# Banded attention: values projected once per block of 512 tokens and fetched back through DRAM, GpSimd placing them, and the output product given its own bank behind the turns

## The reference, cut to what matters

```python
x = layernorm(h)                       # [4, 1024, 128]
q, k, v = x @ Wq.T + bq, x @ Wk.T + bk, x @ Wv.T + bv     # 16 heads of 8
# row i sees its own chunk of 10 and the keys from i-25 up to the chunk's start
allowed = (j in chunk(i)) | ((j >= i - 25) & (j < chunk_start(i)))
p = softmax(q @ k.T * 8**-0.5 + where(allowed, 0, -1e30))
h = h + (p @ v) @ Wo.T + bo
```

## Time and profile before

| | |
|---|---|
| median of three runs | 2047.76 us (2047.59 to 2050.64) |
| the profiled execution's own time | 2046.14 us |
| its span in the profile | 2044.3 us |
| mean granted TensorE clock | 0.976 of full speed |
| attention A, first tile to the next layer's first instruction | 35.7 to about 246 us |
| busy share of the span, PE / DVE / ACT / POOL | 95 / 86 / 61 / 72 % |

### The profile page before, as it was taken

The page is one execution under the profiler, slowest core; times in us unless marked ns, Lnnn a source line. Parts: engine busy times, 40 slices in busy tenths (PEclk is TensorE's granted clock), DMA queues, the critical chain, the costliest instruction groups (busy, mean ns, idle before and its releaser), DMA issues. The chain is left out here.

```text
span 2044.3 us, 55129 instructions
## 1 busy us (share of the span) xinstructions
PE 1936.5 (95%) x22048; PEld 1290.8 (63%) x22048; DVE 1755.2 (86%) x2719; ACT 1239.2 (61%) x2213; POOL 1474.8 (72%) x1046
## 2 busy tenths in 40 slices
PE   4999889999879999999999999999999998899998
PEld 2666654444357777777777777777777776544443
DVE  5777788887679999999999999999999997788876
ACT  2455456666546666666666666666666665466665
POOL 2041035656449999999999999999999998256565
PEclk9999879999979999999999999999999999799999
DMA  7322258866230000000000000000000000487672
GB/s 184 120 72 72 70 108 146 149 118 137 48 114 10 17 10 16 11 14 13 9 18 10 13 14 13 14 10 17 6 10 6 10 6 2 86 152 155 133 138 51
DMA packets 99470, 117.44 MB, mean 57 GB/s; under 512 B 31920, under 2 KB 60976, under 8 KB 98288
## 3 DMA queue, kind: packets, MB, share of 16 engines
q1 hardware_dynamic: 97920, 113.42, 25.6%
q10 hardware_dynamic: 1296, 0.50, 0.1%
HBM read 96.32 MB, written 17.57 MB: 56 GB/s over the span
## 5 line engine op out<-in xcount | busy, mean ns | idle before, releaser
L1029 DVE TENSOR_REDUCE head_shift<-head_score 128x64 bf16<-128x1024 f32 x512 | 624.2, 1219 | 80.2 <-PE head_score L813 68.4
L986 ACT ACTIVATE head_ex<-head_score 128x1024 f32<-128x1024 f32 x512 | 524.7, 1025 | 183.4 <-PE head_score L835 181.7
L770 POOL TENSOR_TENSOR head_half<-head_ex 128x1024 f32<-128x1024 f32 x256 | 604.0, 2359 | 40.3 <-ACT head_ex L986 40.3
L1263 POOL TENSOR_TENSOR ffn_sw<-ffn_sg,ffn_wide 128x512 f32<-128x512 f32 x256 | 324.5, 1268 | 311.5 <-ACT ffn_sg L1374 300.2
L1036 DVE TENSOR_TENSOR head_ex<-head_ex,head_recp 128x1536 f32<-128x1536 f32 x256 | 446.7, 1745 | 4.3 <-ACT head_recp L958 4.3
L845 PE MATMUL head_den<-head_half,c_ident 128*128 128x128 f32 x3072 | 385.4, 275 | 2.4 <-POOL head_half L771 2.4
L845 PEld LDWEIGHTS head_den<-head_half,c_ident 128*128 128x128 f32 x3072 | 363.4, 192 | 6.0 <-POOL head_half L771 2.6
L777 POOL TENSOR_TENSOR head_ex<-head_ex,head_recip 128x512 f32<-128x512 f32 x256 | 328.5, 1283 | 21.5 <-ACT head_recip L960 13.8
L835 PE MATMUL head_score<-head_shift,c_identb 128*128 128x512 bf16 x1024 | 309.9, 384 | 18.1 <-DVE head_shift L1029 12.0
L813 PE MATMUL head_score<-att_b_HB,att_b_GR 96*128 96x256 f16 x2048 | 311.0, 274 | 0.5 <-ACT head_ex L986 0.5
L828 PE MATMUL head_outp<-head_ex,att_b_vs 128*32 128x128 f32 x8192 | 276.5, 276 | 0.6 <-DVE head_ex L1036 0.6
(11 more groups left out here) (255 smaller groups left out, 2545.4 us busy)
## 6 DMA issues: line engine op xcount, KB each, us to landing
ffn_wide<-pair_weights SPq DMA_DIRECT2D x256, 256.0 KB, 9.7
att_b_vs<-in_zero_f SPq DMA_DIRECT2D x2, 2176.0 KB, 9.3
a_keys<-band_parts_k SPq DMA_DIRECT2D x14, 295.5 KB, 2.6
att_a_HB<-a_keys SPq DMA_DIRECT2D x56, 73.9 KB
a_queries<-band_parts_q SPq DMA_DIRECT2D x14, 271.5 KB, 3.0
att_a_GR<-a_queries SPq DMA_DIRECT2D x14, 271.5 KB
b_queries<-head_parts_q SPq DMA_DIRECT2D x32, 96.0 KB, 1.6
att_b_HB<-b_queries SPq DMA_DIRECT2D x128, 24.0 KB
```

The source lines that it names most:

```text
L770: ch.link(pool.tensor_tensor(hf, e[:, 0:8, :], e[:, 8:16, :], ALU.add))
L986: act.activation(ex[:, kt % RING, :, h * QS:(h + 1) * QS], score[:, h, :, :].rearrange("p k (a w) -> p (k a) w", a=NH // 2), ACT.Exp, scal ...
L1029: dve.tensor_reduce(shift[:, h, :], score[:, h, :, :].rearrange("p k (a w) -> p w k a", a=NH // 2), AX.XY, ALU.max, negate=True).then_inc( ...
L1263: pool.tensor_tensor(sw[:, unit % 2, :], sg[:, unit % 2, :], wide[:, k % 2, i, :], ALU.mult).then_inc(sw_ready, 1)
```

## The change

- `values` is called once for a block of 512 tokens (128 columns of `xnT` as weights, 12 matmuls), for blocks 0 to 2 before the first tile and for blocks 3 to 7 in the turns of tiles 3, 6, 9, 12 and 15. The columns of `a_WvT` are reordered on the host, so that even and odd heads lie apart.
- ACT, between the exponentials and the copies of the turned ones, moves them to `v_rows` in SBUF, two instructions with zeros kept between the heads, and writes them to a DRAM tensor `v_dram` of 1 KB a token (ACT's queue). SP reads them back, two DMAs for a group, with 64 keys on 64 partitions and 12 windows in 512-byte pieces, into `v_windows`. POOL copies a tile's 512 elements on each of 128 partitions into `vw`. DVE's `place_values` and the per-tile `values` go.
- On PE, `project`, `turn_x` and `values` come before `turn`, and `output` comes last, into `bank_v`. `project` and `turn_x` no longer wait for `added`.
- `project` runs for 12 groups and not 14, and SP places 12. `place` waits for the group before's reads in front of its writes, not behind its own reads.
- POOL clears all three `HB`/`GR` buffers, adds the bias row block by block between placements, and scales and splits the later weights in 13 pieces (tiles 16 to 28 and 20 to 32), where it did it in four.
- Before the first tile: SP holds back input blocks 3 to 7 until the `a_` weights have landed, `normalise(2)` comes before the low part of the weights, and the bias row is made at the end of DVE's list.

```diff
 # sync
+            def place_windows(n):
+                first = n // NGRP * S + n % NGRP * GT * QT
+                sp.wait_ge(v_written, ONE + blocks_for(first + (WINDOWS - 1) * SUBQ + KWIN) * 16)
+                if n > 0:
+                    sp.wait_ge(v_placed, ONE + n * 32)
+                if n > 1:
+                    sp.wait_ge(v_done, ONE + (n - 1) * GT)
+                for e in range(2):
+                    rows = bass.AP(v_dram.tensor, first * 2 * E + e * E, [[2 * E, KWIN], [SUBQ * 2 * E, WINDOWS], [1, E]])
+                    sp.dma_start(v_windows[e * KWIN:(e + 1) * KWIN, n % 2, :, :], rows).then_inc(v_placed, 16)
...
-            clear(0)
+            sp.wait_ge(a_loaded, ONE + 4 * 16)
             for k in range(EARLY, NBLK):
                 load_x(k)
-            clear(1)
...
-            for n in range(2, B * NGRP + 2):
-                place(n, n % NGRP)
+            for n in range(2, GROUPS):
+                place(n)
+                place_windows(n)
 # gpsimd
+            def place_values(tile):
+                buf, n = tile % GT, tile // GT
+                pool.wait_ge(v_placed, ONE + (n + 1) * 32)
+                if tile >= GT:
+                    pool.wait_ge(att_ready, ONE + tile - GT + 1)
+                slots = vw[:, buf * NSUB * NG:(buf + 1) * NSUB * NG, :].rearrange("p s (r w) -> p s r w", w=16)
+                heads = v_windows[:, n % 2, buf * NSUB:(buf + 1) * NSUB, :].rearrange("p j (g r w) -> p (j g) r w", g=NG, r=2)
+                pool.tensor_copy(slots[:, :, 0:3:2, :], heads).then_inc(v_done, 1)
 # tensor: the turn
                     take_maximum(tile)
-                    values(b, (t + 1) * QT if t < NQT - 1 else S, tile + 1, bank_v)
-                    if out_tile(t) is not None and not (first and t == 0):
-                        output(b, t)
-                    turn(tile)
-                    if block_at(tile) is not None:
-                        pe.wait_ge(added, ONE + outs_before(b, t + 1))
-                        pe.wait_ge(low_ready, ONE + units_before(b, t))
-                        turn_x(block_at(tile))
-                    if t % GT < 2:
+                    if projects(b, t):
                         group = t // GT + 2
                         ahead = group // NGRP * S + group % NGRP * GT * QT
-                        pe.wait_ge(added, ONE + outs_before(b, t + 1))
                         pe.wait_ge(low_ready, ONE + units_before(b, t))
                         pe.wait_ge(xlow_ready, ONE + turned_before(tile))
                         project(b * S + (ahead + (0 if t % GT else LEFT)), KCOLS if t % GT else QCOLS, bank_q, t % GT)
+                    if block_at(tile) is not None:
+                        pe.wait_ge(low_ready, ONE + units_before(b, t))
+                        turn_x(block_at(tile))
+                    if values_at(tile) is not None:
+                        pe.wait_ge(added, ONE + outs_before(b, t) - (1 if t == 0 else 0))
+                        values(values_at(tile), bank_v)
+                    turn(tile)
+                    if out_tile(t) is not None and not (first and t == 0):
+                        output(b, t)
 # scalar
+            def take_values(k, bank):
+                if k > 1:
+                    act.wait_ge(v_written, ONE + (k - 1) * 16)
+                act.wait_ge(v_ready, ONE + k + 1)
...
+                for e in range(2):
+                    places = v_rows[:, k % 2, :, e, :].rearrange("p t (h w) -> p t h w", w=2 * D)[:, :, :, e * D:(e + 1) * D]
+                    heads = bank.rearrange("p (t e h d) -> p t e h d", t=TB, e=2, d=D)[:, :, e, :, :]
+                    last = act.activation(places, heads, ACT.Copy, scale=1 / ASCALE)
+                last.then_inc(v_taken, 1)
+                if k > 0:
+                    act.wait_ge(v_written, ONE + k * 16)
+                act.wait_ge(v_taken, ONE + k + 1)
+                rows = v_dram[LEFT + k * BLK:LEFT + (k + 1) * BLK, :].rearrange("(t p) e -> p t e", p=P)
+                act.dma_start(rows, v_rows[:, k % 2, :, :, :].rearrange("p t e w -> p t (e w)")).then_inc(v_written, 16)
...
+                    if values_at(tile) is not None:
+                        take_values(values_at(tile), bank_v[:, :])
```

More of the change, by code:

```diff
@@ L198, in block_at, with values_at, projects @@
             return EARLY + tile // GT if tile % GT == GT - 1 and EARLY + tile // GT < NBLK else None
+        def values_at(tile):
+            return EARLY + tile // GT - 1 if tile % GT == 0 and tile > 0 and EARLY + tile // GT - 1 < NBLK else None
+        def projects(b, t):
+            return t % GT < 2 and b * NGRP + t // GT + 2 < GROUPS
         def out_tile(t):
@@ L251, in _ @@
             sp.dma_start(whole("a_bo"), drams["a_bo"].partition_broadcast(P)).then_inc(out_loaded, 16)
-            for n in range(2):
-                place(n, n)
+            clear_rows(0, LEFT)
+            clear_rows(LEFT + T, VTAIL)
+            place(0)
+            sp.wait_ge(out_loaded, ONE + 5 * 16)
+            place_windows(0)
+            place(1)
+            place_windows(1)
             for name in LATE:
@@ L293, in project, with values @@
                 product(pe, bank[:, 0:cols], w, u, xh, xl).then_inc(qk_ready, 1)
-            def values(b, first, tile, bank):
+            def values(k, bank):
                 w = c["a_parts"]
-                pe.wait_ge(v_done, ONE + tile)
-                pe.wait_ge(xlow_ready, ONE + blocks_for(b * S + first + (NSUB - 1) * SUBQ + KWIN))
-                for j in range(NSUB):
-                    at = bass.ds(b * S + (first + j * SUBQ), KWIN)
+                pe.wait_ge(xlow_ready, ONE + k + 1)
+                for j in range(TB):
+                    at = slice(LEFT + k * BLK + j * P, LEFT + k * BLK + (j + 1) * P)
                     high, low = xnT[:, 0, at], xnT[:, 1, at]
-                    out = bank[0:KWIN, j * E:(j + 1) * E]
+                    out = bank[:, j * E:(j + 1) * E]
                     pe.matmul(out, high, w[:, 2, 0, :], start=(j == 0), stop=False, skip_group_check=True)
@@ L484, in _ @@
             high_turned(1)
-            for g, banks in enumerate(((bank_q, bank_v), (num, den))):
-                for u in range(2):
-                    high_part(g, g, u, banks[u])
-                if g == 0:
-                    high_turned(2)
+            high_part(0, 0, 0, bank_q)
+            high_part(0, 0, 1, bank_v)
+            high_turned(2)
+            take_values(0, turned[:, 0, :])
+            high_part(1, 1, 0, num)
+            high_part(1, 1, 1, den)
+            take_values(1, score[:, 0, :])
+            take_values(2, score[:, 1, :])
             root(1, slice(EARLY * TB, NT))
@@ L564, in batch @@
                         low_turned(block_at(tile - 1))
-                    if t % GT > 0:
+                    if t % GT > 0 and projects(b, t - 1):
                         low_part(b * NGRP + (t // GT + 2), (par + t // GT) % 2, t % GT - 1, bank_q)
@@ L622, in _ @@
             deviation(1, slice(EARLY * TB, NT))
-            place_values(0, 0, turned[:, 0, :])
+            dve.wait_ge(values_out, ONE + 1)
+            dve.tensor_tensor(c["a_out"][:, :], c["a_bo"][:, :], turned[:, 1, 0:E], ALU.add).then_inc(a_done, 1)
             batch(0, 0, True)
```

169 lines of the change are left out of this document (91 added, 78 removed).

## The result

| | before | after |
|---|---|---|
| median, both timed in turns on one chip (six executions of the change) | 2050.39 us | 2037.36 us (2032.99 to 2041.74) |
| ratio, 95% interval | | 0.9943 [0.9927, 0.9958] |
| profiled execution, its span | 2046.14, 2044.3 us | 2041.47, 2039.7 us |

The change gives 13.0 us, faster as forecast, but about half of the 25 us.

What follows compares the result with a forecast made beforehand. No engine is full; a cycle of waits through PE, DVE and ACT bounds the turns. Turns 19, start 4.1 and end 2.0, about 25 us, take 2046.14 to 2021; forecast for the median 2022.5 us, range 2008 to 2039.

Steps and rivals of the forecast that it cites:

- Start: Before the first scores: held-back input blocks and reordered DVE work were to save 4.1 us, between 2 and 5.5.
- End: From the last tile to the next stage: no reads for an unused group and a shorter last tile, 2.0 us gained.
- plain turn: Turn of a group's first tile, without values: 4.6 us against 5.34, gain 0.75.
- with a low part before a projection: Turns at t = 4 and 7, where PE's projection awaits the low part: 4.9 us against 5.81, gain 0.9.
- third tiles: Third tile of a group, low part delaying attT: 4.8 us against 5.34, or 4.9 against 5.8 with a turned block.
- values turns: Turns of tiles 3, 6, 9, 12 and 15, with twelve values matmuls: 5.85 us against 5.86, nothing gained.
- The exposed normalisation: Four DVE instructions (1.1 us), no longer hidden behind PE's tail at tiles 4, 7 and 13: 3.3 us lost.
- port exclusion: Rival, 12%: DVE's five normalisations in the loop each wait for a POOL placement, at most 6.8 us; 2029 to 2031.
- windows too late: Rival, 8%: SP's serial list delivers windows late, so POOL and attend wait; slower than before, 2075 to 2240 us.
- Costed at nothing, with their cover: Step taking POOL's placements, SP's queue, window reads, late weights and the values' DMA as hidden, at no cost.
- The late weights: Weights issued about 5 us earlier share DMA engines with place(2), wanted at tile 6: nothing to 5 us, taken as nothing.
- DVE and ACT as the bound: Rival, 18%: output last chains addition, statistics and next maxima with PE; turns take 5.2 us, not 4.75: 2038 us.

Runs made afterwards that it cites:

- one window of twelve: The change, but from the third group on each read of the windows fetches 1 of 12 windows, so most tiles use stale values: 2020.05 us.
- windows behind the landed reads: The change, with SP waiting until a group's queries and keys have landed before it issues the window reads: 2029.58 us.
- the kernel before with its reads at the change's pitch: The kernel before, with two unused reads a group added directly behind its own, from rows 1 KB apart: 2048.50 us, ratio 0.9999.
- both cures: The change with window reads in three parts a group, landings not awaited, and the late weights in quarters: 2018.89 us, ratio 0.9856.
- Spreading the weights alone: The change with the late weights in four quarters, issued behind the attends of tiles 1, 4, 7 and 10: 2028.02 us.
- windows by tile: The change with a group's window reads in three parts, each issued after a tile's attend, no landing awaited by SP: 2023.97 us.
- before with the same reads: The kernel before with two input reads a group added into a buffer nobody reads: 2049.08 us behind a wait, 2050.48 us without it.
- half of the numerators' matmuls: The change with all its traffic, but half of the 64 numerator matmuls left out in every attend: 2014.23 us.
- output first: The output product put ahead of the transposes again: 2039.99 us on the change, 2027.38 us with paced windows and quartered late weights added.

## Why the prediction was half right

**Right: the mechanism and its terms.** Start 4.1 forecast, 4.7 measured. End 2.0 and 2.4. In turns that no stall disturbs (of the change and of the kernel with one window of twelve): plain turn 4.6 and 4.52, or 4.73 where a sequence begins; with a low part before a projection 4.9 and 4.52 to 4.75; third tiles 4.8 and 4.52 to 4.55, or 4.73; t = 1 4.65 and 4.31; values turns 5.85 and 5.55. The exposed normalisation, forecast at 1.1 in tiles 4, 7 and 13, shows as turns of 5.44 in tiles 8 and 14, and not in 4 and 7. In the kernel with one window of twelve these add up to 21.3 us in the turns, and that is net of 6.4 lost in tiles 5 and 6 (18.2 us against 11.8 before): the other turns gave 27.7, so the forecast 19 was too small, the first turn (7.55 to 5.53, forecast 1.0) and those with a low part above all. Some 2 us are given back behind attention A: from the next stage's start to the end it is 1800.8 us after and 1798.8 before, 0.6 of it in attention B and most of the rest in the second feed-forward. That was not followed up, and over the variants it scatters: 1798.9 with windows behind the landed reads, 1801.2 in the kernel before with its reads at the change's pitch.

**Right: three rivals put low.** DVE and ACT were no bound: at 4.52 us the transposes wait for ACT by 0.53. POOL's copy takes 0.61 us, not 1.35, and DVE's normalisations keep to 341 ns, as in the earlier trace rows. That does not test the prediction's port exclusion: in the trace after none of the 32 normalisations runs under a GpSimd instruction, so the rule is neither shown nor refuted here, and it cost nothing. The window reads were never late for GpSimd in a way that reached PE, except where I made SP wait for each (2055 us, the "windows too late" rival at a milder price). Of that rival's own prices 2240 counts each group over 16.9 us and 2075 over 14.3; over 16.9 the second is about 2046.

**Wrong: the step "Costed at nothing, with their cover".** Two of its sentences failed.

- "The window reads ... take 3.5. They are wanted four turns after they could start." I took the traffic's cover from its consumer. It has a second user of the same DMA engines: PE's own instruction stream. The size was not far off: 768 KB at 0.2 MB/us are 3.9 us. But the reads go out back to back with `place`'s and land after 6.4 us, and the unbroken burst holds a packet of 256 instructions back for longer than those in hand last. Price: 17.3 us, by the kernel with one window of twelve.
- "The late weights ... from nothing to 5 us, I take nothing." The writes of `place(2)` went out at 49.96 us behind 3 MB of weights, its reads at 62.89, and tile 6 started at 68.75, 10.7 us after tile 5, the turn after it at the slow clock. The forecast has 4.9 and 5.85 us for tiles 5 and 6, the trace 10.68 and 7.59: 7.5 us lost, above the upper bound of 5, with a stall for instructions of 2.23 us among them. In the kernel with both cures these two turns are 4.2 us shorter. Spreading the weights alone gave 9.3 us (8.0 by the ratios), and on top of spread windows 5.1; so this price overlaps with the first.

The range, 2008 to 2039, holds 2037.36, and that is luck: its upper end stood there for DVE and ACT as the bound (2038), which they were not, and no rival named the instructions.

**What is shown, what is argued.** Shown: the loss goes with the traffic's shape (one window 17.3 us, windows by tile 13.4, both cures 18.5), not with its bytes (before with the same reads: nothing); each stall stands at the end of a packet's 256 instructions and ends 1.2 to 1.7 us after the next packet has landed; fewer PE instructions at equal traffic end nearly all stalls. Argued only: that a short turn is what makes the change sensitive. For it: the kernel before spends 5.3 to 5.8 us on some 244 instructions and bears a burst of 5.7 us. Counted in the traces, 256 instructions last at least 5.0 us there, 4.4 in the kernel with one window of twelve and 5.6 with half of the numerators' matmuls; the next packet's delay, its transfer and the 1.2 to 1.7 us behind it have to fit into that. Against its being all: with output first the change needs 4.80 to 5.33 us for 220, no more a microsecond than before, and still has 9.2 us of stalls. The rest should be the longer burst, 6.4 against 5.7 us to landing: with the reads directly behind, packets in the kernel before started at most 4.0 us after PE had begun the 256 instructions before and in the change up to 7.3, counted from 75 us on, behind the late weights. And stalls shrink with the burst (6.4 us to landing: 16.3; 5.9: 14.6; 5.3: 8.5; by tile: 3.7). **Open:** why the change's reads take 0.7 us longer than equal ones in the kernel before; pitch is excluded, the memory they come from (a tensor written in the run, against the input) was not tried. Nor was the values' write on ACT's queue taken out, which runs beside the reads in front of the stalls that end at 100.3, 114.3 and 137.3 us; with one window of twelve it stays and no stall of over 0.45 us is left behind tile 5.

## What to carry over

When a change shortens PE's turns and adds or bunches DMA traffic, look for PE's idle time named "issue" in the middle of a list of equal matmuls, and for the instruction queue's packet at the end of a burst: the instructions come through the same DMA engines as the data. Counting settles it: waits for instructions lie a multiple of 256 of PE's instructions apart. A wait on a DMA queue that seems to cost only time may have been what kept bursts apart; when it goes, cut the transfers to one tile each and release them by the work's own progress, never by each other's landing. A transfer's cover must be asked for every user of the DMA engines, not only for its consumer.

## What the runs showed of the hardware

- A burst in which SP's queue took up to 121% of the sixteen DMA engines in 512-byte pieces kept a 16 KB instruction packet back to the burst's end; PE then stood 0.9 to 3.6 us, at places a multiple of 256 of its instructions apart, and went on 1.2 to 1.7 us after the packet's end.
- In the trace after, the stalls of 1.56 to 3.62 us behind tile 10 brought some 3.4 to 6.8 us at the lower level of the clock (16 score matmuls 1.04 us, not 0.63), so that a stall of 1.82 us cost 2.9. The one of 1.05 us did not.
- 512-byte pieces moved at about 0.2 MB/us in such bursts; with 1 KB pieces (0.22 MB/us) the same bytes landed in 5.9 us in place of 6.4.
- GpSimd's copy of 128x512 float32 elements, written in runs of 16, took 0.61 us. That is 1.2 ns an element and partition, against 2.6 for its scaling.
